# Rotary partner rows by a vector-engine shuffle, gates on ScalarE, new instruction orders

## The reference

```python
# layer 0
x = x + gate_a[:, None] * (attn_out @ W_proj + b_proj)
x = x + gate_m[:, None] * (gelu(h) @ W_mlp2 + b_mlp2)
# layer 1, queries and keys of both attentions
def _rope(t):
    t1, t2 = t[..., :half], t[..., half:]          # half = 4 of 8 features of a head
    return concatenate([t1 * cos - t2 * sin, t2 * cos + t1 * sin], axis=-1)
```

## Time and profile before

| | us |
|---|---|
| median of 3 runs | 383.75 |
| lowest and highest | 380.84 and 387.33 |
| the profiled execution's own time | 385.06 |
| its span, first to last instruction | 383.3 |

### The profile page before, as it was taken

The page is one execution under the profiler, slowest core; times in us unless marked ns, Lnnn a source line. Parts: engine busy times, 40 slices in busy tenths (PEclk is TensorE's granted clock), DMA queues, the critical chain, the costliest instruction groups (busy, mean ns, idle before and its releaser), DMA issues.

```text
span 383.3 us, 12514 instructions
## 1 busy us (share of the span) xinstructions
PE 363.0 (95%) x5090; PEld 260.6 (68%) x5090; DVE 301.7 (79%) x809; ACT 254.5 (66%) x513; POOL 100.6 (26%) x120
## 2 busy tenths in 40 slices
PE   7699999999999999999999999999999899999996
PEld 3485687677776776657654567666677577886776
DVE  5985989999999998947999839997799747875302
ACT  2525965578676987889453797378766945688551
POOL 6920310142020201125351234343413401031130
PEclk9966999999999999999999999999999957999999
DMA  8673244005221360014050140403140404000003
GB/s 208 259 240 93 78 140 167 9 27 186 84 88 43 127 219 5 3 32 169 2 193 6 29 168 7 169 5 106 65 168 4 168 8 159 8 3 3 2 0 111
DMA packets 19757, 34.13 MB, mean 89 GB/s; under 512 B 2740, under 2 KB 7988, under 8 KB 19700
## 3 DMA queue, kind: packets, MB, share of 16 engines
q1 hardware_dynamic: 19268, 33.24, 25.2%
q10 hardware_dynamic: 432, 0.09, 0.2%
HBM read 6.51 MB, written 1.05 MB: 20 GB/s over the span
## 4 chain that ended last, share of the span: by engine, by line
PE 55%; DVE 4%; ACT 3%; DMA 3%; SPq 3%; issue 2%; ACTq 0%; DVEq 0%
PE ps_ao L1058 11%; PE ps_misc L999 8%; PE ps_misc L1028 6%; PE ps_misc L1109 6%; PE ps_misc L1087 6%; PE ps_misc L1025 6%; PE ps_misc L935 3%; PE ps_misc L1094 3%; DVE maxima L690 3%; PE ps_misc L1068 2%; PE ps_misc L1007 2%; ACT PT L882 2%; DMA Ks<-Kl 2%; DMA Ks<-Kh 1%; SPq L537 1%
## 5 line engine op out<-in xcount | busy, mean ns | idle before, releaser
L690 DVE TENSOR_REDUCE maxima<-ps_misc 128x4 f32<-128x512 f32 (+1 forms) x256 | 153.5, 664 | 17.6 <-PE ps_misc L1025 17.1
L882 ACT ACTIVATE PT<-ps_misc 128x512 f32<-128x512 f32 (+1 forms) x256 | 131.7, 606 | 24.0 <-PE ps_misc L1028 22.7
L1058 PE MATMUL ps_ao<-PT,V 120*18 120x128 f32 (+1 forms) x2048 | 70.5, 282 | 0.5 <-ACT PT L882 0.5
L1025 PEld LDWEIGHTS ps_misc<-Ks,Qd 32*128 32x128 f32 x1024 | 41.9, 197 | 30.8 <-issue 11.3
L1025 PE MATMUL ps_misc<-Ks,Qd 32*128 32x128 f32 (+1 forms) x1024 | 53.4, 298 | 8.5 <-DMA Ks<-Kl 3.3
L1058 PEld LDWEIGHTS ps_ao<-PT,V 120*18 120x18 f32 (+1 forms) x2048 | 52.6, 101 | 7.4 <-issue 2.3
L1028 PEld LDWEIGHTS ps_misc<-Qd,Ks 32*128 32x128 f32 (+1 forms) x1024 | 38.0, 186 | 21.5 <-issue 13.7
L752 POOL TENSOR_SCALAR vareps<-mv 128x4 f32<-128x4 f32 (+1 forms) x28 | 6.4, 228 | 170.9 <-DVE mv L595 170.6
L1028 PE MATMUL ps_misc<-Qd,Ks 32*128 32x128 f32 (+1 forms) x1024 | 48.7, 287 | 1.5 <-DVE maxima L690 0.8
L866 ACT ACTIVATE xnT<-ps_misc,vec 128x128 f32<-128x128 f32 x80 | 30.1, 462 | 15.6 <-PE ps_misc L935 15.5
L999 PE MATMUL ps_misc<-xnT,Wr 128*128 128x512 f32 x72 | 37.5, 641 | 1.8 <-ACT xnT L866 1.6
(11 more groups left out here) (83 smaller groups left out, 449.7 us busy)
## 6 DMA issues: line engine op xcount, KB each, us to landing
Qd<-Qh SPq DMA_DIRECT2D x32, 256.0 KB
Ks<-Kh SPq DMA_DIRECT2D x16, 256.0 KB, 2.9
Qd<-Ql SPq DMA_DIRECT2D x16, 256.0 KB
Ks<-Kh SPq DMA_DIRECT2D x16, 240.0 KB, 2.4
Ks<-Kl SPq DMA_DIRECT2D x8, 256.0 KB, 3.0
Ks<-Kl SPq DMA_DIRECT2D x8, 240.0 KB, 2.5
x<-x_in SPq DMA_DIRECT2D x4, 256.0 KB, 6.0
W<-weights SPq DMA_DIRECT2D x2, 512.0 KB, 5.0
```

What stands on the lines that cost most here:

```text
L690: dve.tensor_reduce(maxima[:, h, st.b % HB, c, :], bank(use + c)[:, 0:NG * ns].rearrange("p (n k) -> p n k", n=NG), AX_X, ALU.max, negate= ...
L882: act.activation(PT[0:ns, k % PSLOTS, c, :, :].rearrange("p n t -> p (n t)"), bank(use + c)[0:ns, :], ACT.Exp, scale=SCALE).then_inc(S["pr ...
L1025: ins = pe.matmul(bank(st.use + c)[:, n * ns:(n + 1) * ns], queries, keys, start=True, stop=True)
L1058: last = pe.matmul(ps_ao[32 * c:32 * c + PAIR, block * P:(block + 1) * P], heads[:, at:at + PAIR], PT[0:ns, k % PSLOTS, c, n, :], start=no ...
```

## The change

- The second product of every rotary `k` and `q` step goes, with its weights' columns. DVE makes the cosine product as before and then a `stream_shuffle` of the same bank into `ropeB` that exchanges the halves of each group of 32 partitions. POOL multiplies `ropeB` by the signed sine before it adds.
- POOL lays out four rotary weights where it laid out eight.
- `gate` runs on ACT: the same sum is written as gate times value plus (gate times bias), and DVE makes the two products of gate and bias once.
- `ORDER` is new for all five engines, `BANK` too. `BESIDE` has 15 places with 22 copies; at `max` and `score` steps the identity product comes after waiting for all four banks.

```diff
+TURNED_ROWS = [(i + TROWS // 2) % TROWS for i in range(TROWS)]
-GATES = "dve"
+GATES = "act"
 BESIDE = {
-    "xT.0": 3, "xT.1": 1, "xT.2": 1, "xT.3": 1, "mT.0.0": 1, "norm.0.1": 1, "aT.0": 1, "norm.1.1": 1, "aT.1": 1,
...
+    "xT.1": 2, "xT.2": 2, "mT.0.0": 3, "o.1": 1, "norm.2.1": 2, "norm.7.0": 1, "out.7": 1, "norm.8.0": 1,
+    "norm.9.0": 1, "max.11.0": 1, "xT.12": 2, "xT.13": 1, "out.11": 1, "norm.12.0": 2, "out.12": 1,
 }
-RW = ["k0", "q0", "k1", "q1", "k2", "k2s", "q2", "q2s", "k3", "k3s", "q3", "q3s"]
+RW = ["k0", "q0", "k1", "q1", "k2", "q2", "k3", "q3"]
 ORDER = {
-        warm.0 mods.0 xT.0 k.0 q.0 xT.1 mods.1 q.1 k.1 max.0.0 v.0 max.0.1 v.1 max.0.2 xT.2 mT.0.0 xT.3 max.0.3 k.2
+        mods.0 warm.0 xT.0 mods.1 k.0 q.0 xT.1 v.0 xT.2 k.1 q.1 xT.3 v.1 max.0.0 max.0.1 v.2 max.0.2 q.3 max.0.3
...
                     use = plan.at["pe", st.name].use
-                    for i, dst, table in ((0, ropeA, "cos"), (1, ropeB, "sin")):
-                        dve.wait_ge(S["misc_filled"], use + i + 1)
...
+                    dve.wait_ge(S["misc_filled"], use + 1)
+                    dve.tensor_tensor(ropeA[:, int(not k), 0:n].rearrange("p (b t) -> p b t", b=CB),
+                                      bank(use)[:, 0:n].rearrange("p (b t) -> p b t", b=CB),
+                                      const("cos")[:, None, 0:ns].to_broadcast([P, CB, ns]),
+                                      ALU.mult).then_inc(S["rope_read"], 1)
+                    dve.stream_shuffle(ropeB[:, int(not k), 0:n], bank(use)[:, 0:n],
+                                       TURNED_ROWS).then_inc(S["rope_read"], 1)
...
+                        dve.wait_ge(S["vec_ready"], NV)
+                        for v, gate, name in ((ADD_A, GATE_A, "o0"), (ADD_M, GATE_M, "b2_0")):
+                            dve.tensor_scalar(vec[:, :, v], vec[:, :, gate], bcol(name), None,
+                                              ALU.mult).then_inc(S["adds_ready"], 1)
...
-                            ins = dve.tensor_scalar(yT_sb[:, n % 2, b * P:(b + 1) * P], src[:, b * P:(b + 1) * P],
-                                                    add, vec[:, c, gate:gate + 1], ALU.add, ALU.mult)
...
-                        pool.tensor_tensor(total, total, ropeB[:, int(not k), 0:n],
-                                           ALU.add).then_inc(S["rope_sums"], 1)
+                        pool.tensor_tensor(blocks, blocks,
+                                           const("sin")[:, None, 0:n // CB].to_broadcast([P, CB, n // CB]),
+                                           ALU.mult).then_inc(S["rope_turned"], 1)
+                        rope_sums_made += 1
+                        pool.wait_ge(S["rope_turned"], rope_sums_made)
+                        pool.tensor_tensor(total, total, turned, ALU.add).then_inc(S["rope_sums"], 1)
...
+                            ins = act.activation(yT_sb[:, n % 2, b * P:(b + 1) * P], src[:, b * P:(b + 1) * P],
+                                                 ACT.Identity, scale=vec[:, c, gate:gate + 1],
+                                                 bias=vec[:, c, add:add + 1])
...
-                        for i, form in enumerate(forms):
-                            fill(st.use + i)
-                            pe.matmul(bank(st.use + i)[:, 0:n], w_rows(f"{st.kind}{st.a}{form}"), src[:, 0:n],
-                                      start=True, stop=True).then_inc(S["misc_filled"], 1)
+                        fill(st.use)
+                        pe.matmul(bank(st.use)[:, 0:n], w_rows(f"{st.kind}{st.a}"), src[:, 0:n], start=True,
+                                  stop=True).then_inc(S["misc_filled"], 1)
```

More of the change, by code:

```diff
@@ new lines @@
+        score.2.2 mT.3.0 q.4 norm.2.0 cT.1 score.2.3 value.2.2 max.3.2 xT.5 value.2.3 max.3.3 v.5 norm.2.1
+        score.3.0 q.5 max.4.0 mT.3.1 aT.2 k.5 score.3.1 max.4.1 value.3.0 score.3.2 max.4.2 mT.4.0 value.3.1
+        score.3.3 o.2 max.4.3 value.3.2 value.3.3 score.4.0 yT.2 norm.3.0 mT.4.1 cT.2 score.4.1 norm.3.1 v.6
+        max.5.0 aT.3 value.4.0 score.4.2 max.5.1 value.4.1 score.4.3 value.4.2 max.5.2 mT.5.0 k.6 o.3 max.5.3
+        value.4.3 xT.6 norm.4.0 norm.4.1 score.5.0 q.6 yT.3 mT.5.1 aT.4 cT.3 score.5.1 out.4 k.7 score.5.2
@@ new lines @@
+        norm.7.1 max.8.1 h.m2.2 h.m2.0 max.8.2 aT.7 h.m2.1 out.7 max.8.3 mT.8.0 h2.m2 v.9 max.9.0 xT.m3 max.9.1
+        yT.m2 mT.8.1 h.m3.2 h.m3.3 max.9.2 h.m3.0 h.m3.1 score.8.0 mT.9.0 h2.m3 max.9.3 xT.10 value.8.0 yT.m3
+        score.8.1 q.10 k.10 score.8.2 score.8.3 value.8.1 score.9.0 v.10 mT.9.1 xT.11 value.8.2 norm.8.0 q.11
+        value.8.3 score.9.1 norm.8.1 k.11 value.9.0 score.9.2 max.10.0 aT.8 max.10.1 value.9.1 out.8 score.9.3
+        value.9.2 max.10.2 mT.10.0 value.9.3 max.10.3 norm.9.1 k.12 v.12 v.11 score.10.0 mT.10.1 norm.9.0 xT.12
@@ new lines @@
+        max.11.0 value.10.0 max.11.1 aT.9 k.13 score.10.1 out.9 q.12 score.10.2 mT.11.0 value.10.1 max.11.2
+        value.10.2 score.10.3 norm.10.0 v.13 max.11.3 value.10.3 xT.13 k.14 norm.10.1 score.11.0 q.13 mT.11.1
+        score.11.1 value.11.0 max.12.0 aT.10 max.12.1 value.11.1 score.11.2 out.10 max.12.2 score.11.3 mT.12.0
+        value.11.2 max.12.3 norm.11.0 value.11.3 score.12.0 norm.11.1 v.14 k.15 aT.11 xT.14 max.13.0 mT.12.1 out.11
+        score.12.1 max.13.1 value.12.0 q.14 score.12.2 mT.13.0 xT.15 max.13.2 value.12.1 score.12.3 norm.12.0
@@ L224, in __init__ @@
         self.engine = engine
-USES = {"k": 2, "q": 2, "max": HG, "score": HG, "value": 0, "warm": 0}
+USES = {"max": HG, "score": HG, "value": 0, "warm": 0}
 def uses_of(st):
-    if st.kind in ("k", "q"):
-        return 2 if ATTN[st.a]["rope"] else 1
     return USES.get(st.kind, 1)
@@ L334, in block_kernel @@
         silu = sb("silu", [P, 3, B])
[L335 removed]
+        vec = sb("vec", [P, B, NV + 2])
         x = sb("x", [P, STREAMS, CB, D])
@@ L1011, in _ @@
                         ns = ns_of(st)
+                        taken = st.name in BESIDE
+                        if taken:
+                            for c in range(HG):
+                                fill(st.use + c)
+                            keep_going(st)
                         if st.kind == "max" and st.b == 0:
@@ L1021, in _ @@
                                 queries = Qd[rows, st.f % KSLOTS, n, st.b * P:(st.b + 1) * P]
-                                if n == 0:
+                                if n == 0 and not taken:
                                     fill(st.use + c)
```

226 lines of the change are left out of this document (106 added, 120 removed), and 2 rows, old and new, of the table BESIDE.

## The result

The changed kernel takes 417.55 us (median of 4 runs, 414.87 to 420.75) against 383.4 for the kernel before, run beside it: a ratio of 1.092, 95% interval 1.079 to 1.105. The forecast was 371 us, and faster. The profiled execution took 414.87 us, with a span of 413.1 and a mean granted clock of 0.926, where before had 383.3 and 0.964.

A forecast was written before the change was run, and what follows sets the result against it. PE was taken to bound the kernel, DVE close behind between 40 and 160 us. 385.06 - 13.8 - 3 + 1.1 + 3 = 372.4 us profiled, so 371 predicted; range 362 to 376, for all cases 360 to 384.

The forecast's parts named there:

- The rotary products: Units 8 to 15: 16 key and query steps each lose one 0.86 us product on PE, -13.8 us; at least 0.
- The distances: PE work between hand-overs: 11.3 to 14.6 us (units 8 to 11), 9.0 to 14.0 (12 to 15); 2.3 us needed score to value.
- Shorter hand-overs: Value steps waiting for four exponentials of their score: 15 of 64 pairs short instead of 5, +3 us.
- The slower rival: Values need 3.4 us after their score instead of 2.3, since ACT works in order: +22.8, 393.9 us; chance 0.11.
- Gates: Eight gates move from DVE to ACT: 10.9 us leave DVE, 12 us go to ACT; -3 us taken.
- POOL's chain: Sixteen sine products of 1.28 us on POOL lengthen the rotary chain, covered by PE work: 0; uncovered 10.2 us.
- The shuffle: DVE trades a 0.686 us product for a shuffle taken as 0.69 us, 16 times: 0, from -3.2 to +11.0.
- DVE takes what PE gives: Rotary stage: slower shuffles or normalizations stretched beside POOL keep the stage as long, 381 us; chance 0.14.
- Unit 14: Moves wait for score.12.3's slot; less PE work before max.14.0 makes the wait 2.9 us: +1.1 us.
- Head: Before the first max: DVE's statistics of three streams delay keys, value products and turns fill the wait; 0, -4 to +3.
- One more stretch at 1.2 GHz: Rival case: PE's clock drops once more, costing 6.5 us, 377.5 us; chance 0.08 shared with an uncovered rotary chain.
- four signs: Shuffle over 1 us; PE waiting over 10 us for exponentials; third lower-clock stretch; first max step after 23 us.

The follow-up runs named there:

- old orders: Changed kernel's arithmetic (shuffle, POOL sine product, gates on ScalarE) with step orders and 30 identity copies of the kernel before: 402.89 us, ratio 1.056.
- the shuffle alone: Kernel before, its orders and gates on VectorE kept, with one product and a shuffle per rotary step and POOL's sine product: 396.82 us, ratio 1.041.
- with the sine off POOL: Kernel before with one product and a shuffle per rotary step, its orders and gates kept, sine product on VectorE instead of POOL: 388.19 us, ratio 1.012.
- the run with the products back: Changed arithmetic in the order of the kernel before, but PE makes each rotary product twice into the same bank: 408.73 us, ratio 1.068.
- order-alone run: Kernel before with gates on ScalarE and both rotary products; new orders and banks only before unit 8's first product: 409.25 us, ratio 1.072.
- new then old: Changed kernel's arithmetic throughout; its order and banks up to unit 8's maxima, those of the kernel before behind: 426.65 us, ratio 1.121.
- the control: Kernel before, arithmetic and orders unchanged, with 37 more identity copies at nine steps where PE stood still: 381.72 us, ratio 1.002.
- the filled run with the sine on VectorE: Kernel before with shuffle instead of second rotary product, sine product on VectorE, and 91 identity copies planned at 25 PE stops: 389.62 us, ratio 1.022.
- the fillings: Changed kernel with 41 more identity copies at steps where PE stood still (414.25 us), then 83 more after a second filling (417.97 us).
- the one with both changes in old orders: Changed arithmetic in the order of the kernel before, with 68 more identity copies at steps where PE stood still: 390.11 us, ratio 1.017.

## Why the prediction was wrong, point by point

- *The rotary products, -13.8 us, "nothing beside them hides them".* This step failed. PE's 96% in that stage was read as "PE sets the length". In old orders, where nothing but the rotary arithmetic and its banks differs, the shuffle alone gave +14 us, and with the sine off POOL still +5. In that last run the work went (7.8 us less busy time in the stage), and 10.1 us more of standing still came in its place. Read from the waits, the pairs were cover: behind them ran normalizations, roots and moves of keys, which now end later than PE does. That they were cover is argued, not shown by a run of its own, since the run with the products back was slower still. The bound "at the least it is 0, if another engine sets that stage's length" pointed the right way, and was not low enough: the new chain made hand-overs later besides.
- *The sum had no term for the order of units 0 to 7*, only 0 for the head and -3 for gates. This is the larger failure: 20 to 21 us by unit 8's first `max` step, and 16 to 24 us of the whole time, shown by the order-alone run and by new then old against old orders. The distances were worked out for units 8 to 15 and for score to value alone. Unit 4 shows what they left out: its moves wait for `score.2.3`, and `max.4.0` stands in the new order too close behind it: PE has 7.7 us of work between the two (8.2 before), and the last move lands 9.7 us after that score. In the changed kernel's timeline:

```profile
97.84 0.66 PE L1043 MATMUL ps_misc<-Ks,Qd 32*128 32x120 f32 x16 [2.00 <-DMA Qd<-Qh]
```

- *Shorter hand-overs, +3.* The kind was wrong: value steps wait for 0.3 us. The `max` and `score` steps that take a bank which an exponential or a maximum still holds wait for 14.0 us (2.6 before). The slower rival (393.9 us, chance 0.11) pointed to the right side by the same wrong hand-over, and was 24 us short.
- *Gates, -3.* They cost some 10 us in old orders, and nothing can be told of them in the new ones (421.60 with them back on VectorE against 417.55, whose runs overlap). DVE's 6.8 us off the fullest stage bought nothing that shows.
- *POOL's chain, 0.* Right in the new orders (3 us, with runs that overlap); the old ones lose 5 to 9 us to it. The distances that the prediction added up may have been a good guide there, or other waits hide the chain; no run tells these apart. *The shuffle, 0*: right in size, 0.73 us, but the sum had no term for the bank that it holds (2.1 us at `score` steps in old orders). *DVE takes what PE gives* fell as a sum, since DVE's share is lower than before; its normalizations beside POOL did stretch in old orders, from 28.3 to 34.1 us.
- *Unit 14, +1.1.* No wait at `max.14.0` is left in the changed kernel; PE came there late enough. *Head, 0 (-4 to +3)*: the first `max` step starts 7 us later (26.2 against 19.3), outside the range, but giving the old head back did not help.
- *The clock.* "One more stretch at 1.2 GHz, 6.5 us" was priced as a rival by itself. There are 61 us at the lower level in place of 28, and they come with the stops. No run shows half a stretch as its price: in the control and in the filled run with the sine on VectorE some 20 us at the lower level went, and no time came back, though copies were added for it.
- *Its own signs.* Three of its four signs of being wrong came: PE waits for exponentials for 11.4 us over all its rows, seven stretches at the lower clock show, and the first `max` step starts at 26.2 us. Only the shuffle stayed under 1 us.

What stays open: which rule of the new order makes units 0 to 7 stop so often. That banks come free late is what the waits say; no run moved single steps to show it. Nor could the clock be held in the new orders (0.926, then 0.930 and 0.931 with the fillings), so its 17 us there are worked out from the records, not shown by a run. What the single changes cost in old orders (14 and 10 us) and the order of units 0 to 7 (16 or more) add up to more than the 34 us measured, so the shares in the changed kernel are not known. No version tried beats the kernel before.

## What to carry to other kernels

An engine at 95% in a schedule of tight hand-overs is full, but its work may cover what the others hand over: before counting a removed operation as saved, ask what runs beside it and would be late without it. A new hand-written order is a change of its own, in every unit it touches, and deserves a run with the old arithmetic before anything else is judged. Count the distance from each release (bank, slot, key) to its next user, for all units, not only for those whose arithmetic changes.

## What the runs showed of the hardware

In the changed kernel each of the seven stretches at PE's lower clock begins within 3 us behind a stop of 0.6 to 2.0 us. Not every stop brings one: up to 26.2 us PE stands still for 10.3 us, 6.5 of them at a time, and the clock there is 1.00. The wait of 2.00 us that ends at 97.84 is followed by the longest stretch:

```profile
100.00:117.00 17.00, 15.77 (x201) 10.78 (x203) 10.78 (x27) 9.15 (x20) 2.51 (x3) 0.50 0.14 51
```

With ten copies of the identity in that wait the stretch was gone, and a new one began in another wait, of 2.81 us up to 65.36 (L1049 is the `max` step there):

```profile
64.00:77.00 13.00, 10.99 (x108) 7.92 (x108) 6.84 (x15) 5.28 (x10) 0.00 (x0) 0.50 0.14 47
100.00:117.00 17.00, 15.46 (x233) 10.67 (x234) 11.87 (x23) 10.23 (x21) 0.00 (x0) 1.00 0.32 109
...
65.36 0.91 PE L1049 MATMUL ps_misc<-Ks,Qd 32*128 32x128 f32 x12 [2.81 <-DMA Ks<-Kl]
```

The Trainium skill (TensorE: Matmul & The Clock Gate, A second HAM failure mode: psum-queue depth-cycling) tells of a kernel whose clock swings because PE pauses briefly as it cycles through banks. The trace agrees in part: four of the seven stretches begin behind a wait of 0.6 to 1.0 us for a bank, the longest behind a wait for keys.

The clock also goes with the spread of the kernel before: beside the control it took 378.21 us at a mean clock of 0.991 and 383.83 at 0.969. The control's five runs at 0.990 took 380.07 to 381.01, some two to three us more than before's two at 0.991, so 37 copies cost about as much as the better clock gives back. Filling stops with idle products paid in one kernel of four, the one with both changes in old orders. In two others the clock rose and the time did not fall, and in the changed kernel the clock hardly rose.
